# A Flamingo-style two-layer block on one Trainium2 core: the token table of the expert routing is built by two wide VectorE operations instead of sixteen small ones

## The reference, cut to what matters

```python
probs = softmax(logits)                      # tokens x experts
topk_val, topk_idx = top_k(probs, 2)
y[t] = sum over the two k of  w[t,k] * down_e( silu(gate_e(x[t])) * up_e(x[t]) ),  e = topk_idx[t,k]
out = x + tanh(g_ffn[n]) * y                 # layer 1 adds a shared expert
```

## Time and profile before

| | |
|---|---|
| median of 3 runs | 560.87 us (559.91, 560.87 and 2458.62) |
| the profiled execution, its own time | 564.37 us |
| its span, first to last instruction | 562.5 us |
| mean granted TensorE clock | 0.895 of full |
| PE busy | 457.0 us (81%) |
| PE weight loads busy | 367.6 us (65%) |
| VectorE busy | 369.1 us (66%) |
| ScalarE busy | 171.5 us (30%) |
| GpSimd busy | 136.8 us (24%) |
| share of the chain that ended last | PE 58%, issue 16%, DVE 12%, POOL 8%, DMA 3% |

### The profile page before, as it was taken

One profiled execution on the slowest core, in us unless ns is written; L12 is line 12 of the kernel. 1 busy time (PEld: TensorE's weight loads), 2 busy tenths in 40 slices (PEclk: granted clock), 3 DMA queues, 4 the chain that ended last, 5 costly groups with the idle time before them and its releaser, 6 DMA issues.

```text
span 562.5 us, 8968 instructions
## 1 busy us (share of the span) xinstructions
PE 457.0 (81%) x2894; PEld 367.6 (65%) x2894; DVE 369.1 (66%) x969; ACT 171.5 (30%) x412; POOL 136.8 (24%) x146
## 2 busy tenths in 40 slices
PE   4599999999999997366994479999899755999900
PEld 4368667766766897245873368888799643788800
DVE  5988889888988854733554647668865574455632
ACT  2234232232213602012540135565531101455400
POOL 4815101100110000064406302221100007452073
PEclk9889999999999999567998579999999669799955
DMA  7302211220122061023535204420057103467243
GB/s 258 120 1 75 76 32 44 75 75 3 71 73 73 1 238 62 2 85 94 151 104 163 65 2 144 129 93 19 2 188 298 37 2 102 108 155 134 85 114 110
DMA packets 27424, 51.48 MB, mean 92 GB/s; under 512 B 5184, under 2 KB 16832, under 8 KB 27392
## 3 DMA queue, kind: packets, MB, share of 16 engines
q1 hardware_dynamic: 23264, 39.79, 20.8%
q0 software_dynamic: 4128, 11.28, 8.7%
HBM read 40.83 MB, written 10.22 MB: 91 GB/s over the span
## 4 chain that ended last, share of the span: by engine, by line
PE 58%; issue 16%; DVE 12%; POOL 8%; DMA 3%; another core or an unknown queue 1%; ACT 1%; POOLq 0%; SPq 0%; DVEq 0%
PE ps L861 10%; PE ps L673 8%; PE ps L521 7%; PE ps L523 7%; PE ps L522 7%; POOL qc L502 5%; PE ps L886 4%; POOL probs L473 2%; PE ps L569 2%; PE ps L827 2%; PE ps L621 2%; PE ps L542 2%; PE ps L579 1%; PE ps L871 1%; DMA W<-attn 1%
## 5 line engine op out<-in xcount | busy, mean ns | idle before, releaser
L486 POOL DMA_INDIRECT qb<-stream_rows,gather_rows x54 | 51.5, 953 | 175.5 <-DVE gather_rows L1393 141.1
L473 POOL TENSOR_TENSOR probs<-probs,rowrec 128x512 f32<-128x512 f32 x28 | 28.6, 1043 | 165.4 <-DVE rowrec L1224 165.4
L861 PE MATMUL ps<-experts_s,ring 128*128 x216 | 61.2, 409 | 5.9 <-issue 5.4
L1186 DVE TENSOR_TENSOR big<-ps,big 128x512 fp32r<-128x512 f32 (+3 forms) x80 | 46.6, 629 | 20.9 <-ACT big L932 20.7
L932 ACT ACTIVATE big<-ps 128x512 fp32r<-128x512 f32 (+3 forms) x80 | 41.1, 564 | 59.3 <-PE ps L579 53.9
L1435 DVE SCALAR_TENSOR_TENSOR silu<-silu,ps 128x128 f32<-128x128 f32 x62 | 17.7, 286 | 60.4 <-ACT silu L1083 34.8
L521 PE MATMUL ps<-xs_hi,A_hi 128*128 128x512 f32 x128 | 53.4, 417 | 4.4 <-DVE xs_lo L1181 4.4
L521 PE MATMUL ps<-big 128*128 128x256 f32 (+3 forms) x172 | 52.3, 304 | 0.0
L523 PE MATMUL ps<-big 128*128 128x256 f32 (+3 forms) x172 | 51.7, 301 | 0.0
L522 PE MATMUL ps<-big 128*128 128x256 f32 (+3 forms) x172 | 51.7, 301 | 0.0
L522 PE MATMUL ps<-xs_lo,A_hi 128*128 128x512 f32 x128 | 51.5, 402 | 0.0
(11 more groups left out here) (140 smaller groups left out, 934.1 us busy)
## 6 DMA issues: line engine op xcount, KB each, us to landing
experts_s<-ffn SPq DMA_DIRECT2D x24, 384.0 KB, 5.5
expert_rows<-G SPq DMA_DIRECT2D x54, 128.0 KB
W<-attn SPq DMA_DIRECT2D x8, 704.0 KB, 4.1
W<-attn SPq DMA_DIRECT2D x8, 672.0 KB, 4.2
W<-attn SPq DMA_DIRECT2D x16, 320.0 KB, 4.3
stream_rows<-qb SPq DMA_DIRECT2D x16, 128.0 KB, 1.8
X<-x SPq DMA_DIRECT2D x4, 256.0 KB, 5.3
out<-X SPq DMA_DIRECT2D x8, 128.0 KB
```

The lines of the kernel that those rows point to most:

```text
L473: nc.gpsimd.tensor_tensor(part, part, rowrec[:, 4 * h:4 * h + 4, :].unsqueeze(3).to_broadcast([P, 4, 2, L]), ALU.mult).then_inc(s.p, 1)
L486: nc.gpsimd.indirect_dma_start(XG[:, u, :], None, rows_d[n], bass.IndirectOffsetOnAxis(gather_rows[:, b:b + 1], 0)).then_inc(xg_landed[u], 16)
L861: last = nc.tensor.matmul(psum[GU_BANK + u][:, 0:GU], rows[c], cols[c], start=(c == 0), stop=(c == NCH - 1))
L1186: V.tensor_tensor(dst, src, upper.bitcast(F32), ALU.subtract).then_inc(done, 1)
```

## The change

Of the 16 pairs of small VectorE instructions, the 16 that build `token_hot` go. Two wide instructions over all 128 x 512 elements take their place: one compares the float counter (`lists`, 32 columns repeated for every use) with the block numbers, the other multiplies the result in place with the token numbers. They stand in the middle of the 16 `row_hot` instructions, after those of tiles 0 to 3. The first of them is linked, so DVE waits for it. The semaphore `hot` rises once after the second wide instruction, and then once per tile for tiles 4 to 7. PE's `rows_of_slots` waits once for tiles 0 to 3 together and once for each of tiles 4 to 7.

```diff
-        FF_COUNTS = dict(rows=16 * NT, logits=2, mask=1, rank=1, hot=NT, table=1, ids=1, at=1,
+        FF_COUNTS = dict(rows=16 * NT, logits=2, mask=1, rank=1, hot=1 + NT // 2, table=1, ids=1, at=1,
...
                     for t in range(NT):
-                        pe.wait_ge(*s.hot(t + 1))
+                        if t == 0 or t >= NT // 2:
+                            pe.wait_ge(*s.hot(max(1, t - NT // 2 + 2)))
...
-                    for t in range(NT):
+                    blocks = [NT, 2, 32]
+                    for t in range(NT // 2):
                         for k in range(2):
-                            V.tensor_scalar(row_hot[:, t, k, :], count128, block_row[:, 1, t, k:k + 1], None, ALU.is_equal)
-                            last = V.tensor_scalar(token_hot[:, t, k, :], count32, block_row[:, 0, t, k:k + 1],
-                                                   token[:, t:t + 1], ALU.is_equal, ALU.mult)
+                            last = V.tensor_scalar(row_hot[:, t, k, :], count128, block_row[:, 1, t, k:k + 1], None, ALU.is_equal)
+                    link(V.tensor_tensor(token_hot, lists[:, P:P + 32].unsqueeze(1).unsqueeze(1).to_broadcast([P, *blocks]),
+                                         block_row[:, 0].unsqueeze(3).to_broadcast([P, *blocks]), ALU.is_equal))
+                    V.tensor_tensor(token_hot, token_hot, token[:].unsqueeze(2).unsqueeze(3).to_broadcast([P, *blocks]),
+                                    ALU.mult).then_inc(s.hot.sem, 1)
+                    for t in range(NT // 2, NT):
+                        for k in range(2):
+                            last = V.tensor_scalar(row_hot[:, t, k, :], count128, block_row[:, 1, t, k:k + 1], None, ALU.is_equal)
                         last.then_inc(s.hot.sem, 1)
```

## The result

| | before | after |
|---|---|---|
| median | 560.39 us (6 runs) | 555.14 us (6 runs, 549.27 to 558.66) |
| ratio after / before, 95% interval | | 0.989 [0.9854, 0.9926] |
| profiled execution, its span | 564.37, 562.5 us | 554.35, 552.5 us |

A forecast was written before the change was run, and what follows sets the result against it. The routing loop of small VectorE instructions was taken to lie wholly on the chain, 5.76 us per layer. Cutting it to 3.89 saves 1.87 per layer, 3.7 us in all: 560.87 to 557.1 us, range 554.9 to 560.3.

The forecast's parts named there:

- The chain through the loop: Both layers' routing: the chain walks through all 32 small instructions, 2 x 5.8 us, and nothing covers it.
- `row_hot` back to back: Routing loop: each `row_hot` behind another costs 0.16 us, bounds 0.09 and 0.245, though the trace never showed that.
- Rival A: Routing loop: each small instruction costs its full 0.245 us; loop 5.25 us, gain 1.0 in all, 559.8 us; chance 0.08.
- The wide instructions: Routing loop: the two added VectorE instructions last 0.69 us each and cost 0.72 and 0.61 us.
- the objection drawn from that table: VectorE would stream 2 x 512 elements at the slow rate instead of 16 x 32 at the fast one.
- The sum per layer: Routing loop: 5.76 us before, 3.89 after, so 1.87 us saved in each layer.
- PE's tail: Layer 0's table matmuls: PE catches up before tile 4; the tail stays: 0.05 us, a pair of 0.25, the cast.
- What follows: Behind the loop: layer 0's cast, gathers and experts, layer 1's `hidden(1)`, transpose and table come 1.87 us earlier, no new wait.
- B: Expert blocks: PE's clock moves add time at half clock and take the gain back, 561.5 us; chance 0.12.
- C: Layer 1: PE resumes before the clock falls and runs at full clock, up to 2.1 us more, 555.5 us; chance 0.12.
- Rival D: One layer's gain is swallowed in a wait behind the block pipeline, 559.0 us; chance 0.08.
- the last one of the sum: Whole kernel: 2 x 1.87 = 3.7 us, subtracted from the median of 560.87 as from the profiled execution, giving 557.1 us.

The follow-up runs named there:

- e7: Kernel after plus three linked wide multiplications per layer, giving the loop its old length; timed against the kernel before: 559.56 us, ratio 0.9991.
- e8: Kernel after with the wide comparison first and GpSimd multiplying while VectorE does all 16 `row_hot`; against the kernel before: 556.77 us, ratio 0.9936.

## Why the prediction was right in its sum and missed the first comparison

**The chain through the loop.** Right. What came off the loop came off the path up to the cast in every profile, and padding it back takes the gain away (e7).

**`row_hot` back to back, 0.16 us.** Right, 0.16 in both layers. Rival A needed 0.245 and a loop of 5.25 us; 3.93 us was measured to `hidden(1)`. It has fallen. The rule beside it, that the next operation does not start until the pipeline is empty (the Trainium skill, "VectorE: DVE Perf Modes", section "The DRAIN you can't avoid"), does not describe these rows: the next `row_hot` starts 0.085 us before the one ahead has ended. The exception for one that is not held, which the same section makes, does.

**The wide instructions, 0.72 and 0.61 us.** Right to 0.01. Two sources of different types cost nothing: 0.69 us, as in the earlier trace rows. From 256 elements (425 ns) to 512 (0.69 us) each further one costs about 1 ns. That agrees with the 2,293 ns that the Trainium skill, "VectorE: DVE Perf Modes", section "The perf-mode tier table", gives for a `tensor_tensor` of 2,048 f32 elements, but the objection drawn from that table did not come true: a `token_hot` of 32 columns had cost 0.20 us on the chain, and 16 of these are 3.20 us against 1.33.

**The sum per layer, 1.87 us.** Measured 1.84 and 1.83. PE's tail stayed as said: the last pairs of matmuls are 0.32 us apart and the cast follows at the same distance.

**What follows.** PE's idle time before the transpose was 4.01 us (forecast 3.95). ScalarE's tanh was ready at 448.73, 3 us before `hidden(1)`: no new wait.

**Rivals B and C, the clock.** B has not come. In layer 0 the low stretch inside the blocks was shorter, from about 251.5 to 254.9 us instead of the 6.8 us of the earlier trace rows. In layer 1 the windows of the kernel after (us, PE, PEld, DVE, ACT, POOL busy, granted clock, DMA share, GB/s) read

```profile
452.00:453.00 1.00, 0.58 (x11) 0.52 (x12) 0.82 (x4) 0.06 (x1) 0.00 (x0) 0.50 0.00 0
...
455.00:456.00 1.00, 1.00 (x4) 0.70 (x3) 0.40 (x2) 0.28 (x1) 0.69 (x2) 0.50 0.01 4
456.00:457.00 1.00, 1.00 (x6) 0.79 (x5) 1.00 (x3) 0.36 (x2) 0.69 (x2) 0.87 0.42 127
```

C counted on a clock that was full when PE resumed. It was at half all through the loop, at 1.2 GHz, and rose 2.9 us after the cast, where the earlier trace rows has it rise 3.3 us after. Across the profiles these moves fall now here, now there, in kernels with the same code: cast to first combining gather in layer 0 took 57.04, 54.98 and 56.02 us before and 55.80, 57.28 and 55.81 us after; in layer 1 73.82, 72.10, 73.51 and 72.13, 71.77, 73.43. The means differ by +0.3 and -0.7 us. The 2.9 us that the first pair seemed to give in these stretches is their ordinary spread.

The condition of C never arose: in the kernel before the clock had gone up just after the loop's start at 454.22 and was down again when PE resumed, and in the kernel after it did not go up there. The window in which it rose, before:

```profile
454.00:455.00 1.00, 0.81 (x2) 0.09 (x1) 0.96 (x6) 0.15 (x1) 0.00 (x0) 0.66 0.00 0
```

**Rival D, one layer only.** The stretches speak against it, 1.84 and 1.83 us. The totals can't decide: layer 0 alone gave 1.0 ± 1.5 and 0.7 ± 1.8 us, layer 1 alone 3.3 ± 1.4 and 2.5 ± 1.7. Both fit 1.8 each, and a loss of part of layer 0's gain further back isn't excluded.

**The step that failed** is the last one of the sum: "That execution is 3.5 us above the median of 560.87, and the stretches concerned are short and quiet, so I subtract the same from the median." The edited stretches were quiet, but it put everything else at nothing, with "the runs' own spread of 1 us". Measured, the rest was not nothing. The profiled execution fell by 10.0 us where the sum said 3.7; 6.3 us of that are unchanged code, 3.85 of them ahead of the first changed instruction. Executions of the same kernel spread with a standard deviation of 1.8 us (before, 554.0 to 563.3) and 2.4 us (after, 549.3 to 559.3), so with six runs on either side 3.7 us could come out as 5.2. The base was off as well: 560.87 is the median of three runs, one of them 2,458.62 us, and the kernel before has a mean of 559.5. Less 3.7 that is 555.8 us, the mean of the kernel after. The trace of before held the sign of an unquiet start, the small L1167 and L1168 instructions of 2.2 us, though its page does not list them. That a race caused part of the first surplus is shown for the profiled execution, which started 4.4 us early. For the other executions, of which there is no profile, it is only likely.

The prediction also took 2%, or 11 us, for about the least that a measurement of this kernel tells from no change. The intervals here reach 0.2 to 0.5% to either side, some 1.4 to 2.5 us.

## What to carry to other kernels

On VectorE, count small independent instructions by the time until the next one starts, not by their duration, and replace them by wide ones where pitch times number is larger; here 3.2 us became 1.33. Before a gain of a few microseconds is credited to an edit, compare the times of a point ahead of it in both traces, and hold or remove what moves that point. When a tiny VectorE instruction lasts ten times its usual time, look at what GpSimd runs beside it: one wait that put GpSimd's work 1 to 4 us later was worth more than the whole edit, and both together are the best version measured, 547.3 us, 2.2% below the kernel before.

## What the runs showed that I had not expected

- Beside a GpSimd multiplication of 128x1024 in f32 (2.3 to 2.4 us), a 128x4 VectorE instruction with two SBUF inputs takes 2.0 to 2.3 us instead of 0.16; beside the pieces of 128x256, 0.64 us.
- VectorE instructions that read PSUM in one input went on at their usual time in the same stretch: `big<-ps,big` of 128x256 took 0.41 us at 22.66 in the kernel before, beside GpSimd, and 0.42 us at 14.96 in the kernel after, where GpSimd began 0.25 us later.
- A one-input f16 `tensor_scalar` of 128x128 is held up by GpSimd as well: 16 of them took 3.53 us instead of 2.65 (e8).
